# Attention's joining of tiles: two of the four heads weighted on GpSimd instead of VectorE

## What is computed

```
def _L3_gnn_ref(x, Wq, Wk, Wv, Wo, edge_index):
    ...                                         # N_HEADS = 4, D_HEAD = 8
    scores = jnp.einsum('ehd,ehd->eh', q[dst], k[src]) * inv_sqrt_d
    m = jax.ops.segment_max(scores, dst, num_segments=N)
    ...
    e = jnp.exp(scores - m[dst])
    denom = jax.ops.segment_sum(e, dst, num_segments=N)
    msg = jax.ops.segment_sum(e[:, :, None] * v[src], dst, num_segments=N)
    attn_out = msg / jnp.maximum(denom, 1e-16)[:, :, None]
    out = attn_out.reshape(N, N_HEADS * D_HEAD) @ Wo
    return x + out
```

## Time and profile before

| | |
|---|---|
| median of 3 runs | 3360.53 us (3358.59 to 3364.17) |
| the profiled execution: its own time | 3361.14 us |
| its span, first to last instruction | 3359.3 us |
| joining stage, first DVE instruction to last | 3261.70 to 3354.72 us |
| DVE's busy share of the whole span | 88% |
| GpSimd's busy time in the joining stage | 0.00 us |

### The profile page before, as it was taken

One profiled execution on the slowest core, in us unless ns is written; L12 is line 12 of the kernel. 1 busy time (PEld: TensorE's weight loads), 2 busy tenths in 40 slices (PEclk: granted clock), 3 DMA queues, 4 the chain that ended last, 5 costly groups with the idle time before them and its releaser, 6 DMA issues. The chain is left out here.

```text
span 3359.3 us, 58014 instructions
## 1 busy us (share of the span) xinstructions
PE 2785.8 (83%) x19292; PEld 1821.1 (54%) x19402; DVE 2963.1 (88%) x8488; ACT 598.7 (18%) x1500; POOL 2115.2 (63%) x2076
## 2 busy tenths in 40 slices
PE   8898789885589999969997899999999776777752
PEld 5555555553457777746664566666666433333321
DVE  9999999995839999879999788888888389999987
ACT  3110110011410000001110111111111133333320
POOL 0777777774007777757774766777774377777740
PEclk6889988996557888879998899999999788888875
DMA  5111111111321111121112111111111011111120
GB/s 174 33 35 35 34 34 36 35 33 51 106 100 33 25 24 25 16 29 29 29 28 29 33 30 30 31 30 30 30 31 17 14 27 27 27 27 27 27 16 5
DMA packets 142874, 120.20 MB, mean 36 GB/s; under 512 B 64431, under 2 KB 126451, under 8 KB 142467
## 3 DMA queue, kind: packets, MB, share of 16 engines
q0 software_dynamic: 65152, 44.96, 8.7%
q1 hardware_dynamic: 73842, 63.36, 7.7%
q10 hardware_dynamic: 3600, 8.19, 0.6%
HBM read 85.00 MB, written 31.35 MB: 35 GB/s over the span
## 5 line engine op out<-in xcount | busy, mean ns | idle before, releaser
L1682 POOL DMA_INDIRECT flow_x<-node_table,src_indices x440 | 516.6, 1174 | 246.1 <-PE p_x_turned L1798 106.8
L729 PE MATMUL p_in_picked<-block_table 128*96 128x512 bf16 x1725 | 449.6, 425 | 94.4 <-DVE block_table L606 94.4
L606 DVE TENSOR_SCALAR block_table<-in_sources,node_numbers 128x512 bf16<-128x512 f16 x1725 | 520.4, 371 | 0.1
L2049 POOL DMA_INDIRECT att_kv_rows<-kv_table,att_index x440 | 425.4, 967 | 142.3 <-issue 131.0
L1130 POOL DMA_INDIRECT rel_rows<-message_table,message_indices x320 | 324.0, 1013 | 295.7 <-POOLq L1347 198.5
L1822 PE MATMUL flow_acc_bwd<-flow_onehot_j,flow_by_q 128*128 128x270 bf16 (+1 forms) x2530 | 494.0, 325 | 7.2 <-issue 0.2
L429 POOL DMA_INDIRECT sorted_edges<-block_table,sorted_row x416 | 402.9, 969 | 126.7 <-issue 125.8
L729 PEld LDWEIGHTS p_in_picked<-block_table 128*96 128x96 bf16 x1725 | 231.1, 138 | 286.8 <-DVE block_table L606 95.5
L1423 POOL DMA_INDIRECT sum_rows<-node_table,src_indices x280 | 270.6, 966 | 110.4 <-issue 85.0
L2085 DVE TENSOR_REDUCE att_tile_max<-p_att_scores 128x4 f32<-128x512 f32 x440 | 284.0, 683 | 28.2 <-PE p_att_scores L2199 23.8
L1458 DVE TENSOR_SCALAR sum_source_onehot<-sum_sources,node_numbers 128x512 bf16<-128x512 f16 x1000 | 300.7, 366 | 0.0
(11 more groups left out here) (346 smaller groups left out, 4903.4 us busy)
## 6 DMA issues: line engine op xcount, KB each, us to landing
flow_dst_lanes<-dst_rows SPq DMA_DIRECT2D x110, 128.0 KB, 3.0
rel_rows<-sorted_edges SPq DMA_DIRECT2D x20, 572.0 KB, 3.7
in_sources<-source_rows_in SPq DMA_DIRECT2D x69, 128.0 KB
message_table<-message_rows ACTq DMA_DIRECT2D x25, 320.0 KB, 2.2
message_table<-message_rows SPq DMA_DIRECT2D x25, 320.0 KB, 2.1
flow_x<-node_table,src_indices POOLq DMA_INDIRECT x440, 2.6
att_kv_rows<-kv_table,att_index POOLq DMA_INDIRECT x440, 2.5
sorted_edges<-block_table,sorted_row POOLq DMA_INDIRECT x416, 2.2
```

Of the source, the lines that this page charges most:

```text
L606: last = dve.tensor_scalar(which[g % 2][:, c, :], srcs[b][:], s["node"][:, c:c + 1], None, ALU.is_equal)
L729: last = pe.matmul(pp[g % 2][0:3 * F, 0:CW], hs[:, c].rearrange("p k f -> p (k f)"), which[g % 2][:, c, :], start=(c == 0), stop=(c == NB ...
L1682: pool.indirect_dma_start(out=X[b][:, t, 0:F], out_offset=None, in_=d["nodes"], in_offset=bass.IndirectOffsetOnAxis(ap=s["idx_src"][:, g * ...
L2049: pool.indirect_dma_start(out=KV[b][:, t, :], out_offset=None, in_=d["kv"], in_offset=bass.IndirectOffsetOnAxis(ap=ibuf[b][:, t:t + 1], ax ...
```

## The change

Step 3 is no longer cut by tiles but by columns. DVE first multiplies all 4 denominator columns over all 440 tiles (one instruction), then the 16 message columns of heads 0 and 1 over all tiles (one instruction). GpSimd, in a program of its own for this stage, waits for `wexp` and multiplies the 16 message columns of heads 2 and 3 over all tiles (one instruction). Step 4's scans come in a new order: columns 0 to 15, then 32 to 35, then 16 to 31, and before column 16 DVE waits for a new semaphore, `weighed`, that GpSimd's instruction raises.

```
+MINE = 2
...
+            weighed = sem(st2, "join_weighed")
...
                     dve.wait_ge(wexp, 1)
-                    for lo in range(0, T, T // 2):
-                        sl = slice(lo, lo + T // 2)
-                        dve.tensor_tensor(O4[:, sl], O4[:, sl], w[:, sl].unsqueeze(3)
-                                          .to_broadcast([P, T // 2, HEADS, DH]), ALU.mult)
-                        v.done(dve.tensor_tensor(O[:, sl, F:OW], O[:, sl, F:OW], w[:, sl], ALU.mult))
-
-                    for c in range(OW):
+                    dve.tensor_tensor(O[:, :, F:OW], O[:, :, F:OW], w[:], ALU.mult)
+                    mine = DH * MINE
+                    v.done(dve.tensor_tensor(O4[:, :, 0:MINE], O4[:, :, 0:MINE], w[:, :, 0:MINE].unsqueeze(3)
+                                             .to_broadcast([P, T, MINE, DH]), ALU.mult))
+
+                    for c in (*range(0, mine), *range(F, OW), *range(mine, F)):
+                        if c == mine:
+                            dve.wait_ge(weighed, 1)
                         last = dve.tensor_tensor_scan(O[:, :, c], keep[:], O[:, :, c], 0.0, ALU.mult, ALU.add)
...
+                @block.gpsimd
+                def _(pool):
+                    pool.wait_ge(wexp, 1)
+                    pool.tensor_tensor(O4[:, :, MINE:HEADS], O4[:, :, MINE:HEADS], w[:, :, MINE:HEADS].unsqueeze(3)
+                                       .to_broadcast([P, T, HEADS - MINE, DH]), ALU.mult).then_inc(weighed, 1)
```

## The result

| | before | changed |
|---|---|---|
| median, 11 runs each | 3360.53 us (3355.02 to 3373.26) | 3369.32 us (3362.53 to 3375.30) |
| ratio | | 1.0022 (95% interval 1.0013 to 1.0032) |
| profiled execution: its own time, span | 3361.14, 3359.3 us | 3375.30, 3373.5 us |
| first multiplication to end of last scan | 51.91 us | 56.96 us |

In this comparison the change makes the kernel slower, by 0.22%; the interval is 4.4 to 10.8 us. A second comparison, further down, gives 0.12%. The last row of the table is called **the stretch** from here on; its two ends are the start of the first DVE instruction behind the exponentials and the start of the load behind the last scan, less its 0.03 us gap.

What follows compares the result with a forecast made beforehand. DVE alone was taken to bound the joining stage; with exclusion, 9.45 + 15.2 + 0.2 - 17.02 = +7.8 us on 3361.14 gives 3368.9 us (3368.3 against the median), range 3352.5 to 3373.5.

Steps and rivals of the forecast that it cites:

- The bound: Joining stage, multiplications through scans: DVE alone is the chain, so time taken from or added to it changes the program fully.
- What goes from DVE: Joining-stage multiplications: two instructions in place of four, 9.45 us instead of 17.02, so 7.57 us less for DVE.
- Exclusion: Joining stage: DVE instructions with two SBUF inputs and GpSimd's multiplication stop each other for whole instructions; +7.8 us, chance 0.75.
- the two places that it called likeliest: Joining stage: the long DVE instruction is a denominator multiplication at 17 us or a head multiplication at 22 us.
- The cast: Program start, 4.14 us: DVE cast of 416 elements took 3.02 us instead of 0.38 beside a GpSimd memset; evidence for exclusion.
- The order does not matter: Joining stage: wherever GpSimd's instruction gets in, the path carries DVE's 9.45, GpSimd's 15.2 and the scans' 34.89 us.
- GpSimd's price: GpSimd's multiplication of 7040 elements, heads 2 and 3: 15.2 us, range 6.4 to 18.9.
- two reads in turn with the write beside them: Alternative price of GpSimd's multiplication: 1.78 ns per element, 12.7 us; with exclusion +5.3 us, 3365.8 us.
- Handing over: Between GpSimd's and DVE's instructions in the joining stage: at most 0.24 us, taken as 0.2 us.
- The sum: Joining stage: 9.45 + 15.2 + 0.2 - 17.02 = +7.8 us, giving 3368.9 us, or 3368.3 against the median.
- Free running: Rival, joining stage: GpSimd multiplies beside DVE undisturbed, chain 7.57 us shorter, 3353.0 us; chance 0.15.
- turns: Rival, joining stage: engines share the read path element by element, many scans slightly longer, -7.6 to +4.9 us; chance 0.10.

Runs made afterwards that it cites:

- A second comparison: The changed kernel unchanged, measured once more against the kernel before: ratio 1.0012 (1.0001 to 1.0022), median 3366.83 us against 3361.54, stretch 56.94 us.
- GpSimd alone: Changed kernel, but DVE waits for GpSimd's multiplication before its own first one: GpSimd 12.83 us, 57.3 us from exponentials' end to last scan's end.
- all on DVE: Changed kernel, but DVE multiplies heads 2 and 3 too in a third instruction, no GpSimd program in the stage: stretch 51.85 us, ratio to before 1.0005.
- both operands in PSUM: Changed kernel with DVE's weights and the scans' first input `keep` in PSUM, GpSimd's weights in SBUF: stretch 44.2 us, ratio to before 0.9967.
- GpSimd ahead of the scans: From the kernel before: DVE multiplies columns 0 to 3, GpSimd the other 32 by fours; head 0's weights and `keep` in PSUM: stretch 36.85 us, ratio 0.9951.
- one head on GpSimd: Changed kernel with one head instead of two on GpSimd, three on DVE: stretch 54.60 us, median 3367.53 us, ratio 1.0025 (1.0010 to 1.0040).
- the memset experiment: Changed kernel, but DVE does all multiplications in three instructions and GpSimd only memsets 7040 elements of a spare array: stretch 51.82 us.
- The runs with an operand in PSUM: Two variants of the changed kernel: DVE's weights in PSUM, stretch 49.20 us; the scans' `keep` in PSUM too, stretch 44.2 us, ratio 0.9967.
- one input: Changed kernel with a tensor_reduce of the same 7040 elements replacing DVE's multiplication of heads 0 and 1: stretch 49.43 us, reduction 7.48 us.
- GpSimd between, behind and ahead: Changed kernel 56.96 us; GpSimd waiting for DVE's multiplication of heads 0 and 1, 56.91; DVE waiting for GpSimd first, 57.3 from the exponentials' end.

## Why the prediction was right, and where its sizes were off

**The bound.** That the stretch is a single chain on DVE held in nine of the ten further runs; in the one with GpSimd alone, GpSimd's instruction stands ahead of it in the chain, as was meant. That every microsecond there arrives in the kernel's time is borne out only within the medians' scatter: the ratios of the kernels with all on DVE, with both operands in PSUM and with GpSimd ahead of the scans agree with their stretches, that with one head on GpSimd is larger than its stretch explains.

**What goes from DVE.** 7.57 us by the sum; the kernel with both operands in PSUM gained 7.7. The denominators in one piece took 1.99 us, not 1.93: joining the two instructions saved nothing.

**Exclusion.** Right, in one of the two places that it called likeliest: a head multiplication of 20 us that ends one multiplication's length behind GpSimd's. (Its own prices made that one 7.49 + 15.2 = 22.7 us, where it wrote 22.) The step from the earlier trace rows to it was weaker than it read, though. The cast stood behind a memset, and the memset experiment shows that a tensor_tensor does not; what carries the result is the other half of the argument, that of the earlier trace rows, that an instruction with two SBUF inputs needs a second path for reading. The runs with an operand in PSUM show directly that it is the second input in SBUF that collides; that it comes by a path of its own is the reading of this, and fits every run. It was a right conclusion drawn in part from a row on another collision, and to that extent luck. The rule of the Trainium skill (SBUF — State Buffer, Who interferes with whom) held in every point that was tried: two SBUF inputs against a GpSimd instruction that reads SBUF, whole instructions, first come first served (20.05 us instead of 7.41, and GpSimd 14.63 instead of 12.83), one input or a memset not at all (7.48 us).

**The order does not matter.** Right: 56.96, 56.91 and 57.3 us with GpSimd between, behind and ahead.

**GpSimd's price.** This is the term that was mis-sized. The sum took 15.2 us from the memset on scattered elements; the measured instruction takes 12.83 alone. The price of two reads in turn with the write beside them, 12.7 us, which the prediction named and passed over, was the right one in size, though no run shows how GpSimd orders its reads and its write. The row on elements 52 words apart, 2.0 ns each, was a bad guide to runs of 8 adjacent elements, which took 1.8 ns with two inputs. The estimate of 15.5 us by the figure of the Trainium skill (GPSIMD Engine Reference, Elementwise) was too high as well.

**Handing over.** 0.2 us were added; the runs show none. DVE ended 7.35 us after GpSimd, and takes 7.41 to 7.49 alone.

**The sum.** +7.8 us was forecast, the stretch has +5.05, of which the price of GpSimd explains 2.4 and the handover 0.2; the rest is that behind the denominators GpSimd took 12.69 us (3286.74 to 3299.43), a little less than alone. The medians say +8.8 and +5.3 in two comparisons. That the first hit the forecast within 1.0 us is partly the scatter of this kernel: by its own steps the forecast was 2.7 us too high, and with the stretch as it was measured it would have been 3365.6 us, inside the 0.2% that the prediction counts as the same. The second comparison, 0.12%, lies there too. So the mechanism is shown, and that the first median came out beyond 0.2% is in part luck.

**The rivals.** Free running would have had no long DVE instruction; turns would have had many slightly long ones. Both are refuted for operands in SBUF, and the first is what one gets with one operand of each DVE instruction in PSUM.

## What to carry to other kernels

Before work is split between VectorE and GpSimd, look at where VectorE's operands lie: while GpSimd reads SBUF, a VectorE instruction with two SBUF inputs stood still for the whole of GpSimd's instruction. GpSimd needed 1.7 times VectorE's time for the same multiplication, so where VectorE is the whole chain, every element handed over costs time: the stretch was 51.9 us with none of the message columns on GpSimd, 54.6 with a quarter and 57.0 with half. With one input of each of VectorE's instructions in PSUM the split worked as drawn. And two engines that a profile shows as fully busy side by side may be one working and one held up: compare the duration of an instruction with that of the same shape elsewhere.

## What the runs showed of the hardware

- A VectorE multiplication or scan with two SBUF inputs and a GpSimd multiplication exclude each other for whole instructions, in the order in which they start; GpSimd also gets in between two scans that follow each other without a wait (one scan of 36 at 13.64 us). With one input in PSUM, with a reduction, or against a GpSimd memset, there was no effect (7.48 us each time; 36 scans with `keep` in PSUM 34.83 us).
- GpSimd's multiplication of float32 by a broadcast weight took 12.83 us for 7040 elements and 6.7 us for 3520, which is about 1.7 ns per element and 0.6 to 0.7 us of start; 1760 elements in runs of 4 took 3.93 us, spaced 3.89 us apart, a little more than that line gives (3.6 to 3.7).
- A scan of 440 elements costs VectorE 0.97 us, 2.2 ns per element, with its first input in SBUF (36 in 34.89 us) or in PSUM (34.83).
- GpSimd's memset of 7040 adjacent float32 elements took 5.97 us, 0.85 ns each.
